# A causal attention block with a quantised linear layer: the six middle groups of heads written out in place of a loop on the engines

## The reference, cut to what matters

```python
q = _apply_rope((hidden_states @ Wq.T).reshape(B, S, H, D), cos, sin)   # k likewise; v without rope
scores = jnp.einsum('bhid,bhjd->bhij', q, k) * scale
bias = jnp.where(in_band, learnable_bias[:, jnp.clip(diag, 0, MAX_BIAS_LENGTH - 1)], 0.0)
scores = jnp.where(causal[None, None], scores + bias[None], -jnp.inf)
m = jnp.maximum(jnp.max(scores, axis=-1), off)
p = jnp.exp(scores - m[..., None])
denom = jnp.sum(p, axis=-1) + jnp.exp(off - m)
out = jnp.einsum('bhij,bhjd->bhid', p, v) / denom[..., None]
x = _layernorm(x + out.transpose(0, 2, 1, 3).reshape(B, S, Dm) @ Wo.T)
x = _layernorm(x + (quant_dequant_mxfp4(x) @ quant_dequant_mxfp4(weight).T + bias))
```

## Time and profile before

| | |
|---|---|
| median of 3 runs | 1840.67 us (1837.74 to 1841.23) |
| the profiled execution's own time | 1839.2 us |
| its span, first to last instruction | 1837.4 us |
| mean granted TensorE clock | 0.948 of full speed |
| busy: TensorE, VectorE, ScalarE, GpSimd | 90%, 70%, 60%, 14% of the span |
| instructions in the trace | 33402 |

### The profile page before, as it was taken

The page is one execution under the profiler, slowest core; times in us unless marked ns, Lnnn a source line. Parts: engine busy times, 40 slices in busy tenths (PEclk is TensorE's granted clock), DMA queues, the critical chain, the costliest instruction groups (busy, mean ns, idle before and its releaser), DMA issues. The chain is left out here.

```text
span 1837.4 us, 33402 instructions
## 1 busy us (share of the span) xinstructions
PE 1656.6 (90%) x9136; PEld 772.3 (42%) x9136; DVE 1293.5 (70%) x3801; ACT 1108.2 (60%) x1596; POOL 249.4 (14%) x123
## 2 busy tenths in 40 slices
PE   7999999589999998998998998998999998777762
PEld 3444444224444444444444444444444443333331
DVE  2545444497877876886886877877888841689996
ACT  2333333207787786776776876786787787344432
POOL 4233333210000000000000000000000000134443
PEclk9999999759999999998998999999999999899996
DMA  5444443832632633442333432533352302112211
GB/s 204 141 162 139 163 164 134 197 61 48 119 57 48 119 58 49 90 86 49 78 68 59 93 56 50 91 85 49 61 115 47 60 13 75 35 58 69 83 54 46
DMA packets 124680, 157.64 MB, mean 86 GB/s; under 512 B 14929, under 2 KB 80529, under 8 KB 124241
## 3 DMA queue, kind: packets, MB, share of 16 engines
q1 hardware_dynamic: 124496, 155.45, 36.1%
HBM read 104.15 MB, written 50.46 MB: 84 GB/s over the span
## 5 line engine op out<-in xcount | busy, mean ns | idle before, releaser
L878 ACT ACTIVATE probs<-ps 128x1024 f32<-128x1024 f32 (+3 forms) x768 | 590.0, 810 | 222.4 <-PE ps L687 163.2
L1168 DVE CUSTOM_DVE_ANT_0 junk<-ps,bias_q 128x384 bf16<-128x384 f32 (+2 forms) x1024 | 502.2, 503 | 170.8 <-PE ps L662 156.3
L662 PE MATMUL ps<-k_stack,q_stack 96*128 96x384 bf16 (+3 forms) x1536 | 506.9, 347 | 32.8 <-DVE mx L1168 16.3
L681 PE MATMUL ps<-q_stack,k_stack 99*128 99x512 bf16 (+3 forms) x1536 | 496.3, 333 | 25.2 <-issue 12.6
L1161 DVE TENSOR_REDUCE mx<-ps 128x1 f32<-128x128 f32 (+3 forms) x768 | 364.9, 486 | 44.1 <-PE ps L662 37.2
L687 PE MATMUL ps<-bias_r,ident_r 128*128 (+3 forms) x1280 | 358.6, 368 | 13.0 <-issue 13.0
L638 PE MATMUL ps<-attn 128*128 128x512 f32 x768 | 331.6, 594 | 11.9 <-DMA attn<-hT 9.7
L702 PE MATMUL ps<-probs,v_sb 128*32 128x512 f32 (+3 forms) x3072 | 328.3, 499 | 0.1
L662 PEld LDWEIGHTS ps<-k_stack,q_stack 96*128 96x128 bf16 x1536 | 145.1, 98 | 384.0 <-DVE mx L1168 155.3
L687 PEld LDWEIGHTS ps<-bias_r,ident_r 128*128 128x128 f32 x1280 | 226.1, 196 | 52.7 <-issue 15.4
L638 PEld LDWEIGHTS ps<-attn 128*128 128x128 f32 x768 | 146.4, 191 | 196.2 <-issue 196.2
(11 more groups left out here) (90 smaller groups left out, 1070.6 us busy)
## 6 DMA issues: line engine op xcount, KB each, us to landing
q_stack<-q_parts SPq DMA_DIRECT2D x192, 128.0 KB, 4.2
v_dram<-v_sb SPq DMA_DIRECT2D x32, 512.0 KB, 2.7
v_sb<-v_dram SPq DMA_DIRECT2D x32, 512.0 KB, 9.4
q_parts<-q_stack SPq DMA_DIRECT2D x96, 128.0 KB, 1.9
k_parts<-k_stack SPq DMA_DIRECT2D x96, 128.0 KB, 2.0
k_stack<-k_parts SPq DMA_DIRECT2D x32, 384.0 KB, 7.1
attn<-hT SPq DMA_DIRECT2D x8, 1024.0 KB, 5.8
k_stack<-k_parts SPq DMA_DIRECT2D x32, 256.0 KB, 7.9
```

The source lines that it names most:

```text
L662: pe.matmul(ps_ring[:, use.bank, 0:c1 - c0], q_stack[0:STACK, b, hl, I * P:(I + 1) * P], k_stack[0:STACK, b, hl, c0:c1], start=True, stop= ...
L681: mm = pe.matmul(ps_s[:, u % 2, hh, 0:w], k_stack[0:ROWS, b, hl, J * P:(J + 1) * P], q_stack[0:ROWS, b, hl, i0:i0 + w], start=not in_bank, ...
L878: act.activation(probs[:, (u // 2) % 3, 2 * pr:2 * pr + 2, 0:w], ps_s[:, pr, :, 0:w], ACT.Exp).then_inc(exp_done, 1)
L1168: ins = dve.tensor_tensor_reduce(out=junk[:, use.bank, 0:c1 - lo], in0=ps_ring[:, use.bank, lo - c0:c1 - c0], in1=bias_q[:, hl, BAND - t0 ...
```

## The change

The loop on the engines becomes a loop of the program that builds the kernel. `phase2` is built eight times over for each of the four engines, with `g` a plain number each time, so that every count and address is a constant. What is computed, the order of products, all waits and all transfers stay.

```diff
         def groups(eng, body):
 
-            body(0, FIRST_GROUP)
-            with eng.Fori(1, G - 1) as g:
-                body(g, MIDDLE)
-            body(G - 1, LAST_GROUP)
+            for g in range(G):
+                body(g, LAST_GROUP if g == G - 1 else MIDDLE if g else FIRST_GROUP)
```

## The result

The changed kernel takes 1794.35 us (median of 4 runs, 1793.23 to 1794.68) against 1840.59 us before (4 runs). The ratio is 0.9751, 95% interval 0.9734 to 0.9768. The forecast was 1796.6 us in a range of 1792 to 1803.

What follows compares the result with a forecast made beforehand. The prediction took TensorE to bound the middle groups. Gains of 39.05 + 0.23 + 4.8 = 44.1 us put the profiled execution, 1839.2 us, at 1795.1; adding 1.5 gave a median of 1796.6 us, range 1792 to 1803.

Steps and rivals of the forecast that it cites:

- The jumps: Five jumps back between middle groups: idle time and the low clock behind it vanish, gaining 39.05 us.
- TensorE's pause: After each jump back TensorE fetches the loop start's code, which it no longer holds: waits of 2.81 and 2.67 us.
- stand beside TensorE's pause: Jumps of VectorE, ScalarE and SyncE coincide with TensorE's idle time there, so removing them gains nothing of its own.
- The ends of the loop: Entry to and exit from the middle groups' loop: register setup and last compare go, gaining 0.23 us.
- The register arithmetic: Middle batches: without TensorE's register rows the pace falls from 34.55 to 34.35 us, gaining 4.8 us over 24 batches.
- no wait is added or moved: Whole change: the same loads are issued against the same counts, with no wait or transfer added or moved.
- The added code: Written-out middle groups: TensorE fetches some 45 blocks, covered by matmuls queued ahead, costing nothing.
- The group's start: Rival: pauses at group starts come from something a group needs arriving late, and stay: 1835.4 us, 3 in 100.
- The pace that stays: Rival: middle batches stay at 34.55 us and only the jumps are gained: 1801.4 us, 8 in 100.
- The tail's loop: Rival: the last stage's loop shifts within its code block and is fetched anew at four jumps: 1828 us, 4 in 100.
- stall stands in the straight line: Rival: TensorE runs dry at each new block of written-out code, 45 at 2.7 us: 1918 us, 2 in 100.
- The level: Whole kernel: profiled execution forecast at 1795.1 us, with the median of runs 1.5 us above it, hence 1796.6 us.

Runs made afterwards that it cites:

- the run with the body moved: Kernel before, with 24 semaphore increments that nobody reads ahead of TensorE's loop, shifting its body within its code block: 1829.04 us, ratio 0.9953.
- the run with one wait: Changed kernel, where score products of units with seeded bias wait for the seeding alone, not also the earlier exponential: 1789.68 us, ratio 0.9730 to the kernel before.
- the run with kept joints: Kernel before, with each middle group in its own loop of one turn, entered by a branch and left by a compare falling through: 1795.69 us, ratio 0.9775.

## Why the prediction was right, point by point

**The jumps, 39.05 us.** Right in size: without them all middle batches run at the pace of group 0, two jumps in place of five left 15.8 us of joints, and a loop of one turn, which never jumps back, left none. That TensorE's pause is the fetch of code is borne out by the run with the body moved, in which the second pause went and both blocks came in the first. Only in part right was the reading that the pause is TensorE's own. Its jumps alone cost 35 us, and with them gone the others' still cost 20. The prediction wrote that their jumps "stand beside TensorE's pause", which holds, but it left out that they cost 20 us when that cover is gone. Had the change been made on TensorE alone, I would have forecast 1801.3 us on that chip and been 18 us off.

**The ends of the loop, 0.23 us.** The first and last middle batch now take 34.35 and 34.37 us; right.

**The register arithmetic, 4.8 us.** The amount came: 24 batches went from 34.55 to 34.35 or a few hundredths more, and the middle groups took 824.51 us where 824.4 were forecast. The step that failed is whose it is. I worked it out from TensorE's 344 rows. The runs show that with the loop and its registers on VectorE alone the pace is 0.12 us slower, on ScalarE alone 0.16, on all but TensorE 0.28, and on TensorE alone 0.09 *faster*: 0.28 - 0.09 is the 0.20 of the kernel before, within rounding. For VectorE a place of it can be seen. These are the two instructions of the normalising step in batch 6, before and then after:

```profile
633.33 0.25 DVE L1216 RECIPROCAL rden<-den 128x16 f32<-128x16 f32 x1
633.73 0.42 DVE L1219 TENSOR_TENSOR attn<-ps,rden 128x256 f32 x1
```

```profile
631.34 0.25 DVE L1214 RECIPROCAL rden<-den 128x16 f32<-128x16 f32 x1
631.62 0.42 DVE L1217 TENSOR_TENSOR attn<-ps,rden 128x256 f32<-128x256 f32 x1
```

The product begins 0.40 us after the reciprocal began with a register in its address, and 0.28 us with a constant. VectorE's reading of the ring comes later by as much, and so does TensorE's next product for the maxima: it starts 9.83 us into the batch before and 9.70 after. For ScalarE a place can be seen too: in the run with its loop alone the seeding starts 0.56 us into batch 6 and the product that waits for it at 1.50, where the changed kernel has 0.49 and 1.44.

For TensorE, its register rows carried one of two waits, so that the late one hung on the product; the run with one wait gives that back without registers, and more. So "no wait is added or moved" in the prediction was not quite so: no count changed, but the late wait went from the product into a row of its own, at 0.09 us. The forecast of 34.35 came right because group 0, from which it was taken, is written out and has this cost already. The gain of 0.20 us a batch is thus 0.28 from VectorE and ScalarE less 0.09 on TensorE.

Why group 6 of the run with kept joints fell to 34.55 us with no registers stays open. So the 0.20 us are shown to go with the loop on VectorE and ScalarE, but not that nothing else can bring them, and of the registers themselves only the two places above are seen.

**The added code, nothing.** Right: 47 blocks fetched for 45 forecast, no stall among them.

**The rivals.** The group's start as the cause fell with the kept joints (1795.69 us). The pace that stays fell with the result. The tail's loop kept its code: its branch takes a median 208 ns on TensorE as in the earlier trace rows. And no stall stands in the straight line.

**The level.** The measured median is 2.25 us below the forecast, within the spread of the runs of before. 1.2 us of it are the step from the profiled execution to the median, for which the forecast took 1.5 us from the runs of before and which is 0.3 here. The other 1.0 us are in the profiled execution itself. The first stage, whose code is the same in both, took 1.4 us less there (417.24 and 415.86 us), and the tail 0.2 more.

## What to carry to other kernels

A loop on the engines whose start is no longer held when it jumps back pays at every jump. Here TensorE, VectorE and ScalarE each paid: 7.8 us a jump together, 7.0 by TensorE's alone, 4.0 by the other three's. The length of body at which this begins was not measured. Look for a compare-and-branch row of microseconds and for waits put down to issue that occur as often as the loop turns, and take the loop out on all engines that have them, since fixing the busiest one uncovers the rest. Where code is written out already at one end of a loop, its pace tells in advance what the whole will run at. And in a stream of products near the bound, a wait that another one implies is worth taking out: here it gave 4.3 us.

## What the runs showed of the hardware that I had not expected

A branch row on VectorE's or ScalarE's queue does not show the cost of its fetch: in the run with only TensorE written out the rows at the first jump took 56 and 45 ns, while the first VectorE instruction behind it came after 3.36 us for issue. Only TensorE's branch row shows it (median 3325 ns). With the body moved by 24 instructions, the same jump cost one pause of 3.67 us in place of 2.81 and 2.67, and both blocks of code were fetched ahead of the first product instead of one ahead and one behind it. Semaphore increments on TensorE's queue went 0.15 us apart although each row is 51 ns. A late wait in a row of its own let the product start 0.144 us after its release, and 0.056 when it hung on the product. Code written out six times is fetched in fewer packets (47) than the loop that stood for it (64).
